# The low part of the attention probabilities in two instructions of 512 columns on GpSimd, from the tenth pair of heads on

## What is computed

```python
q = (x @ Wq).reshape(b, s, N_HEADS, HEAD_DIM)
k = (x @ Wk).reshape(b, s, N_HEADS, HEAD_DIM)
v = (x @ Wv).reshape(b, s, N_HEADS, HEAD_DIM)
dot = jnp.einsum('bihd,bkhd->bhik', q, k)
w = jax.nn.softmax(dot / jnp.sqrt(jnp.float32(HEAD_DIM)), axis=-1)
a = jnp.einsum('bhij,bjhd->bihd', w, v)
a = a.reshape(b, s, N_HEADS * HEAD_DIM)
return a @ Wo + bo
```

## Time and profile before

| | |
|---|---|
| median of 3 runs | 861.61 us (859.55 to 862.63) |
| the profiled execution | 861.55 us |
| its span in the trace | 859.8 us |
| TensorE busy | 765.1 us (89%) |
| GpSimd busy | 677.8 us (79%) |
| ScalarE busy | 683.3 us (79%) |
| VectorE busy | 543.3 us (63%) |
| L853, 256 instructions | 541.2 us |

### The profile page before, as it was taken

One profiled execution on the slowest core, in us unless ns is written; L12 is line 12 of the kernel. 1 busy time (PEld: TensorE's weight loads), 2 busy tenths in 40 slices (PEclk: granted clock), 3 DMA queues, 4 the chain that ended last, 5 costly groups with the idle time before them and its releaser, 6 DMA issues. The chain is left out here.

```text
span 859.8 us, 22266 instructions
## 1 busy us (share of the span) xinstructions
PE 765.1 (89%) x9180; PEld 527.8 (61%) x9180; DVE 543.3 (63%) x903; ACT 683.3 (79%) x844; POOL 677.8 (79%) x439
## 2 busy tenths in 40 slices
PE   0859999999999999999999899999999862999891
PEld 0326666666666656566666566666656552999790
DVE  4866676666666666666777566666766135765573
ACT  2759998989898989999999889998997954344352
POOL 2788987979787878889898999888999976077741
PEclk9969999999999999999999999999999985899896
DMA  5600319112020303030313122130300022213312
GB/s 174 150 1 2 78 26 190 45 42 58 23 67 13 75 5 76 5 79 2 78 27 87 37 77 62 52 97 16 79 2 5 2 70 63 58 52 88 107 41 86
DMA packets 43138, 49.30 MB, mean 57 GB/s; under 512 B 6785, under 2 KB 27655, under 8 KB 42912
## 3 DMA queue, kind: packets, MB, share of 16 engines
q1 hardware_dynamic: 39872, 43.31, 20.7%
q0 software_dynamic: 2496, 4.24, 1.5%
q10 hardware_dynamic: 672, 0.33, 0.2%
HBM read 14.28 MB, written 9.25 MB: 27 GB/s over the span
## 5 line engine op out<-in xcount | busy, mean ns | idle before, releaser
L853 POOL TENSOR_TENSOR pl<-p,ph 128x1024 f16<-128x1024 f32 x256 | 541.2, 2131 | 77.9 <-ACT ph L756 77.7
L910 DVE TENSOR_REDUCE mx<-mps 128x1 f32<-128x1024 f32 x249 | 304.2, 1222 | 135.0 <-PE mps L597 132.4
L755 ACT ACTIVATE p<-sps,escale 128x1024 f32<-128x1024 f32 x256 | 285.8, 1116 | 58.5 <-PE sps L577 44.5
L756 ACT ACTIVATE ph<-sps,escale 128x1024 f16<-128x1024 f32 x256 | 284.4, 1111 | 0.0
L672 PE MATMUL pair_bank<-v,ph 128*128 128x65 f16 x2048 | 215.8, 193 | 11.3 <-POOL pl L853 8.8
L672 PEld LDWEIGHTS pair_bank<-v,ph 128*128 128x128 f16 x2048 | 191.1, 97 | 49.2 <-POOL pl L853 17.9
L674 PE MATMUL pair_bank<-v,ph 128*128 128x64 f16 x2048 | 215.5, 195 | 0.0
L676 PE MATMUL pair_bank<-v,pl 128*128 128x65 f16 x2048 | 215.1, 193 | 0.0
L674 PEld LDWEIGHTS pair_bank<-v,ph 128*128 128x128 f16 x2048 | 190.7, 97 | 28.2 <-issue 0.3
L576 PE MATMUL sps<-q_hh,k_hl 128*128 128x512 f16 x512 | 195.1, 381 | 10.0 <-ACT ph L756 9.5
L577 PE MATMUL sps<-q_lm,k_h 65*128 65x512 f16 x512 | 195.7, 382 | 0.0
(11 more groups left out here) (250 smaller groups left out, 969.5 us busy)
## 6 DMA issues: line engine op xcount, KB each, us to landing
q_hh<-hi SPq DMA_DIRECT2D x60, 128.0 KB, 2.4
q_lm<-lo SPq DMA_DIRECT2D x30, 128.0 KB, 2.4
k_h<-hi SPq DMA_DIRECT2D x30, 128.0 KB, 2.4
k_hl<-hi SPq DMA_DIRECT2D x29, 128.0 KB, 2.5
k_hl<-lo SPq DMA_DIRECT2D x29, 128.0 KB, 2.5
sorted<-pad SPq DMA_DIRECT2D x1, 2990.0 KB, 19.0
xb<-sorted SPq DMA_DIRECT2D x46, 65.0 KB, 1.9
v<-in_w1T SPq DMA_DIRECT2D x8, 352.0 KB, 3.7
```

The costliest lines, as they stand in the source:

```text
L755: nc.scalar.activation(p32[:, n % 4, :], sps[:, n % 2, :], ACT.Exp, bias=EXP_BIAS, scale=escale[:, 0:1])
L756: nc.scalar.activation(ph[:, n % 4, :], sps[:, n % 2, :], ACT.Exp, bias=EXP_BIAS, scale=escale[:, 0:1]).then_inc(s_exp, 1)
L853: nc.gpsimd.tensor_tensor(pl[:, n % 4, :], p32[:, n % 4, :], ph[:, n % 4, :], ALU.subtract).then_inc(s_subp, 1)
L910: nc.vector.tensor_reduce(mx[:, i // TB, i % TB:i % TB + 1], src, AX.X, ALU.max).then_inc(s_mx, 1)
```

## The change

In `low_parts` the steps below `PCH * (HALF + 1)` = 144 keep the one instruction of 1024 columns. Steps 144 to 255 (pairs 9 to 15, the tenth to the sixteenth) have two instructions, one on columns 0 to 511 and one on columns 512 to 1023; the wait is before the first, and the second raises `s_subp`. In the changed kernel the lines are L854 (whole), L857 (first half) and L858 (second half); everything below moves down by 5 lines.

```diff
--- before.py
+++ after.py
@@ -850,8 +850,13 @@
         def _(pool):
             def low_parts(n):
                 pool.wait_ge(s_exp, n + 1)
-                nc.gpsimd.tensor_tensor(pl[:, n % 4, :], p32[:, n % 4, :], ph[:, n % 4, :],
-                                        ALU.subtract).then_inc(s_subp, 1)
+                if n < PCH * (HALF + 1):
+                    nc.gpsimd.tensor_tensor(pl[:, n % 4, :], p32[:, n % 4, :], ph[:, n % 4, :],
+                                            ALU.subtract).then_inc(s_subp, 1)
+                else:
+                    nc.gpsimd.tensor_tensor(pl[:, n % 4, 0:512], p32[:, n % 4, 0:512], ph[:, n % 4, 0:512], ALU.subtract)
+                    nc.gpsimd.tensor_tensor(pl[:, n % 4, 512:], p32[:, n % 4, 512:], ph[:, n % 4, 512:],
+                                            ALU.subtract).then_inc(s_subp, 1)
 
             nc.gpsimd.memset(mem["ident"][:], 0.0).then_inc(s_zero, 1)
             pool.wait_ge(s_zero, 1)
```

## The result

| | before | after |
|---|---|---|
| median | 861.42 us (859.55 to 862.63, 4 runs) | 867.80 us (866.18 to 868.48, 4 runs) |
| the profiled execution | 861.55 us | 866.18 us |
| its span | 859.8 us | 864.4 us |

The change costs 6.4 us: the ratio is 1.0073, with a 95% interval of 1.0056 to 1.009. I had forecast slower, 864.8 us, in a range of 860.8 to 870.0. The sign and the range held; the size was about half of what came (3.3 us against 6.4).

The account below looks back on a forecast made before the run. TensorE sets the pace in most changed steps, GpSimd in 161 to 171 and 226 to 255; their extras, 0.88 + 2.40 = 3.28 us, added to 861.55 give 864.8 us, range 860.8 to 870.0.

Parts of the forecast that it names:

- The places: Steps 161 to 171 (0.88 us) and 226 to 255 (2.40 us) pass the extra on; other changed steps hide it.
- The price of a split: On GpSimd, two subtractions of 512 columns take 2.17 us, 0.08 us more than one of 1024; range -0.05 to 0.185.
- The signs: Expected traces: pairs 2.17 us apart, 0.36 us gaps near 515 us, last subtraction ending near 701.7 us.
- Steps 213 to 225: GpSimd falls behind but still waits about 0.5 us three times; 0.40 us extra fits, hidden up to 0.10 us a step.
- rival 1: Each instruction carries its whole fixed time, 0.185 us, in the exposed steps, some from 213 to 225 too; 870.0 us, chance 0.15.
- The sum: Over the exposed steps, 0.88 + 2.40 = 3.28 us, passed unchanged to the end of the span; 864.8 us.
- Rival 2: In the same 41 steps the split costs nothing, 0 to -0.05 us a step; 859.5 to 861.6 us, chance 0.24.
- Rival 3: GpSimd becomes the bound everywhere, 0.35 us more for each of 112 splits; about 20 us, 882 us, chance 0.03.
- The rest of the program unchanged: After the last subtraction and its block, the remaining 161 us of the program stay the same.

Follow-up runs that it names:

- the run with quarters: The kernel before with steps 161 to 171 and 226 to 255 each in four instructions of 256 columns; 877.54 us, ratio 1.02.
- the shared steps: The kernel before with steps 161 to 171 and 226 to 255 shared, GpSimd columns 0 to 511, VectorE the rest; 857.19 us, ratio 0.9949.

## Why the prediction was right, and by how much it was off

- **The places.** Right. Steps 144 to 160 and 172 to 212 are hidden (58 splits: ratio 1.0003), steps 161 to 171 and 226 to 255 pass each extra on. The 41 alone give 1.0071, the whole change 1.0073. In the run with quarters the same 41 steps carried three times the extra.
- **The price of a split.** This is the term that failed: "nearest to L875 in operation, types and size, so 0.08 it is". It measured 0.14 to 0.146 (1.52 / 11, 4.23 / 30, 1.61 / 11), and 0.14 from start to start (2.23 - 2.09). I took one neighbour at the right size, and a difference of two nearly equal numbers (2.17 - 2.09) turned its 30 ns into a factor of two: 2 x 0.03 us is the 0.06 that is missing (a half lasts 1156 ns, L875 1125). The row of 8 columns stood in the same list. I used it as an upper end, 0.185 us, and forgot to take off the overlap of 0.04 us that I had just read from L853; with it the row gives 0.145.
- **The signs.** Near 515 us I had forecast gaps of 0.36 us in place of 0.52. There were none: the backlog of steps 161 to 171 lasted until 526.52 us, where the first gap was 0.23 us. The delay from V(144) to the end of the last subtraction is 6.27 us, not 41 times the price of a split (5.7 to 6.0), which I had named as a sign that the stretches were read wrongly; the next point has the difference.
- **Steps 213 to 225.** I put the limit of the cover at 0.10 us a step. At 0.14 it did run out, and 0.4 us were passed on (75.52 and 75.58 us against 75.14 and 75.16), as rival 1's sum had it in kind.
- **The sum.** 41 x 0.14 to 0.146 = 5.7 to 6.0, with the carried 0.4 it is 6.1 to 6.4 us; measured +6.27 in the attention and +6.4 in the medians. The direction did not hang on the price, since every price above zero gives slower. That the range held owes more to rival 1, which set its upper end, than to the forecast's own sum.
- **Rival 1** (the whole fixed time) was nearer than my forecast: 0.185 without the overlap was too much, its steps and its carry were right.
- **Rival 2** (free) is refuted by the 41 steps alone: their interval begins at 1.0053. What it built on, L329's 1.04 us, is an instruction with other operands and says nothing on this one.
- **Rival 3** (GpSimd the bound everywhere) did not come: no engine waited for the subtractions between 495 and 621 us.
- **"The rest of the program unchanged"** holds for the code but not for a single span: V(255) to the end took 159.2 to 164.4 us in the profiles of one chip.

## What to carry to other kernels

Splitting an instruction on the engine that sets the pace costs its fixed time once per additional piece, less the overlap at the hand-over, in every step of a run in which that engine works without a pause until another engine waits for it. Where it idles for longer than the price in each step, the split is free; where it idles for less, the rest is passed on. Take the fixed time from two rows of the same kind of instruction far apart in size, not from one neighbour, when the price is the small difference of large numbers. And here a half was worth having only where another engine took it: signalling it early gained nothing, giving it to VectorE gained 0.5% even though the two engines hindered each other.

## What the runs showed of the hardware

- GpSimd's subtraction of float16 from float32 follows one line over five sizes: 187 ns and 1.90 ns for each column of 128 partitions (430 ns for 128 columns, 675 for 256, 1156 for 512, 1887 for 896, 2131 for 1024). 0.04 us of it overlaps the instruction before, so an additional instruction in a run without a pause costs 0.14 us.
- VectorE with two inputs in the on-chip memory can be shut out over several hand-overs between GpSimd's instructions: 8.1 us for an instruction of 1.28, behind the rest of one, two more and an addition of 4.5 us. In two of the ten profiles with the instruction in this place it got in at the first hand-over and took 1.5 us, and GpSimd's next instruction took 2.11 us in place of 1.13. In the shared steps, with 512 columns, it took 0.67 to 2.28 us, median 0.78.
